# One kernel, two attention layers and two mixtures of experts: new block parts, zeros on another queue, earlier routing, norm rows on ScalarE

## The reference, cut to what is computed

```python
# x: 16 x 256 tokens x 128; 16 heads of 8 dims
x = x + layernorm(softmax_attention(layernorm(x)))       # "soft" layer: q, k, v, o with biases
x = x + layernorm(block0(layernorm(x)))                  # block0 as follows
    h = rmsnorm(X, norm1_w);  X = X + softmax_attention(h) @ wo
    h2 = rmsnorm(X, norm2_w)                             # 4096 tokens
    topw, topi = top_k(softmax(h2 @ router_w), 2)        # 8 experts, 2 for each token
    combine = one_hot(topi) * softmax(topw)
    moe = swiglu(h2, shared) + sum_e combine[:, e] * swiglu(h2, expert e)    # d_ff 256
    return X + moe
x = x + layernorm(power_attention(layernorm(x), W))      # |q.k|^2 with cumulated log gates, causal
x = x + layernorm(capped_moe(layernorm(x)))              # 8 experts, top 2, at most cap tokens each
```

## Time and profile before

| | |
|---|---|
| runs | 1182.12, 1184.04, 1192.7 us; median 1184.04 |
| profiled execution | 1178.53 us, span 1176.7, mean granted clock 0.906 |
| busy, share of the span | PE 1030.3 us (88%), DVE 887.7 (75%), ACT 757.2 (64%), POOL 644.3 (55%) |
| DMA | 75.23 MB in 116022 packets, mean 64 GB/s |

### The profile page before, as it was taken

One profiled execution on the slowest core, in us unless ns is written; L12 is line 12 of the kernel. 1 busy time (PEld: TensorE's weight loads), 2 busy tenths in 40 slices (PEclk: granted clock), 3 DMA queues, 4 the chain that ended last, 5 costly groups with the idle time before them and its releaser, 6 DMA issues. The chain is left out here.

```text
span 1176.7 us, 30894 instructions
## 1 busy us (share of the span) xinstructions
PE 1030.3 (88%) x10524; PEld 615.7 (52%) x10524; DVE 887.7 (75%) x2262; ACT 757.2 (64%) x1638; POOL 644.3 (55%) x707
## 2 busy tenths in 40 slices
PE   4899998999999999885899889888989999938975
PEld 2344444444444444474699765555555566524752
DVE  3899998898898899674544767988888889874223
ACT  1688887888887778831355356757767689733314
POOL 3244444455344444156473647978877678725763
PEclk9999999999999999998899887967777699966998
DMA  5112222212222211001354331111121011132217
GB/s 125 33 47 57 56 56 56 55 52 56 56 56 55 57 43 32 13 24 55 108 149 133 101 86 30 54 51 43 48 61 30 22 47 45 46 133 68 53 61 202
DMA packets 116022, 75.23 MB, mean 64 GB/s; under 512 B 21335, under 2 KB 108064, under 8 KB 115872
## 3 DMA queue, kind: packets, MB, share of 16 engines
q1 hardware_dynamic: 109296, 60.71, 19.1%
q0 software_dynamic: 5888, 12.10, 3.6%
q10 hardware_dynamic: 688, 0.46, 0.1%
HBM read 26.75 MB, written 26.51 MB: 45 GB/s over the span
## 5 line engine op out<-in xcount | busy, mean ns | idle before, releaser
L621 DVE TENSOR_REDUCE mxsS<-scoreS 128x2 f32<-128x512 f32 x512 | 328.6, 685 | 45.7 <-PE scoreS L760 41.2
L509 ACT ACTIVATE PTS<-stS 128x512 f32<-128x512 f32 x512 | 283.5, 592 | 65.8 <-PE stS L764 65.1
L975 POOL TENSOR_TENSOR PTP<-PTP,EP 128x512 f32<-128x512 f32 x128 | 164.7, 1293 | 69.8 <-ACT PTP L1204 68.8
L760 PE MATMUL scoreS<-QK 31*128 31x256 f16 x1024 | 171.3, 280 | 33.5 <-DVE mxsS L621 14.8
L764 PE MATMUL stS<-QK 32*128 32x256 f16 x1024 | 167.9, 277 | 0.9 <-ACT PTS L509 0.9
L685 PE MATMUL pvS<-PTS,Vx 128*32 128x256 f32 x2048 | 140.3, 392 | 0.4
L1396 DVE TENSOR_SCALAR AP<-score_psP 128x768 int32<-128x768 int32 x128 | 121.7, 951 | 21.6 <-PE score_psP L1555 20.6
L1204 ACT ACTIVATE PTP<-AP,epsP 128x768 f32<-128x768 f32 x128 | 119.0, 930 | 25.0 <-DVE AP L1396 24.4
L760 PEld LDWEIGHTS scoreS<-QK 31*128 31x128 f16 x1024 | 53.7, 93 | 154.3 <-DVE mxsS L621 96.3
L382 POOL TENSOR_TENSOR rsS<-veS,halfS 128x2 f32<-128x2 f32 (+1 forms) x32 | 28.0, 874 | 190.2 <-DVE veS L589 103.7
L1216 ACT ACTIVATE EP<-decay_psP 128x512 f32<-128x512 f32 x128 | 75.9, 593 | 49.6 <-PE decay_psP L1537 47.8
(11 more groups left out here) (389 smaller groups left out, 2356.8 us busy)
## 6 DMA issues: line engine op xcount, KB each, us to landing
QK<-HLS SPq DMA_DIRECT2D x384, 32.0 KB, 1.9
QK<-HLP SPq DMA_DIRECT2D x192, 32.0 KB
gsin<-sorted SPq DMA_DIRECT2D x46, 128.0 KB
mixed<-gob SPq DMA_DIRECT2D x46, 128.0 KB, 1.9
sorted<-ggot SPq DMA_DIRECT2D x22, 256.0 KB, 2.4
expert_outputs<-tzero SPq DMA_DIRECT2D x8, 512.0 KB
cgot<-expert_outputs SPq DMA_DIRECT2D x16, 256.0 KB, 5.3
tokens<-XB SPq DMA_DIRECT2D x16, 128.0 KB, 3.1
```

The costliest lines, as they stand in the source:

```text
L509: act.activation(PT[:, n % NPT, :], st_ps[:, (NS * t + n) % 3, :], ACT.Exp, scale=SCALE).then_inc(s_exp, 1)
L621: dve.tensor_reduce(mxs[:, u // 4, :, at], score_ps[:, n % 2, :].rearrange("p (c s) -> p c s", c=TC), AX.X, ALU.max).then_inc(s_max, 1)
L760: scored = pe.matmul(score_ps[:, k, cols], QK[part, new, g, 0, rows], QK[part, new, g, 1, :], start=True, stop=True)
L975: eng.tensor_tensor(w, w, E[:, n % NE, :], ALU.mult).then_inc(s_wd if n % NU in MULT_BY_DVE else s_wp, 1)
```

## The change

- The parts become 3 and 5 blocks: 19 and 27 groups (still 46), 24 and 40 scatters.
- The tables are cleared from ACT's queue: POOL writes a block of zeros at (-3, 0), and ACT issues seven pieces of up to 7 groups at (-3, 0), (-3, 2), (-3, 4), (-2, 0), (-2, 2), (-2, 4), (-1, 0). SP's 24 pieces go.
- Fronts: block 0's goes to soft step 30, blocks 1 and 2 stay in step 31, block 3 moves to units 1 to 3, blocks 4 to 7 some units earlier, on DVE and ACT ahead of the unit's own product and gate. `choose(0)` and `count(0)` are in step 31, `rank(0)` ahead of unit 0 (was unit 2); `choose(1)`, `count(1)`, `rank(1)` are in units 11, 12, 13 (were 14, 15, 16).
- `apply` becomes `shift` (DVE, one 128x4 instruction: minus mean times root), `rows` (ACT, four row scalings with that bias) and `added` (DVE, the add).
- Among the units: block 0 is finished from unit 41 on, blocks 1 and 2 by unit 54, and the head steps of the power layer lie in units 48 to 60. SP's spreads move from 55 and 58 to 51 and 55, its decay spreads from behind the last unit to 59 and 61.
- Block 3 is finished whole in the power layer. Block b of 3 to 7 has its gathers at odd slots of steps 2b-6 and 2b-5, and everything else in step 2b-4: `add0` at slot 0, `add1` 2, `moments` 3, root 4, `shift` 5, `rows` 6, `added` 7.

```diff
-            act.wait_ge(gated.s_sum, 8)
+            act.wait_ge(gated.s_sum, 6)
...
-MOE_PARTS = (4, 4)
+MOE_PARTS = (3, 5)
...
+def nothing_rows(pool):
+    pool.memset(half[:], -0.5).then_inc(s_zero, 1)
+    pool.memset(zero, 0.0).then_inc(s_zero, 1)
+
 def fixed_tables(pool):
-    pool.memset(half[:], -0.5).then_inc(s_zero, 1)
...
-    pool.tensor_tensor(ahead[:], cst[:, C_TRI:C_TRI + P], cst[:, C_IDENT:C_IDENT + P], ALU.subtract)\
-        .then_inc(s_zero, 1)
-    pool.memset(zero, 0.0).then_inc(s_zero, 1)
+    pool.tensor_tensor(ahead[:], cst[:, C_TRI:C_TRI + P], cst[:, C_IDENT:C_IDENT + P], ALU.subtract)
...
 def soft_gpsimd(pool, what, b):
-    if what == "tables":
+    if what == "nothing":
+        nothing_rows(pool)
+    elif what == "tables":
...
 def scatter(pool, h, k):
...
-        pool.wait_ge(s_zero, 3 + 16 * ZERO_PIECES)
+        pool.wait_ge(s_zero, 2 + 16 * ZERO_PIECES)
...
+    moved(0, range(0, 6))
...
-    moved(0, range(0, 4))
+    moved(0, range(6, 9))
...
-    moved(0, range(4, 2 * len(tiles[0])))
+    moved(0, range(9, 2 * len(tiles[0])))
...
-    for b in range(4):
+    for b in range(first_block[1]):
...
+    out_root(pool, first_block[1] - 1)
...
 def front_bank(b):
-    return gate_ps[:, 0, :] if b in (1, 3) else front_ps[:]
+    return down_ps[:, 0, :] if b == 0 else gate_ps[:, 0, :] if b == 2 else front_ps[:]
...
 def turn(pe, b):
...
+        pe.wait_ge(soft.free["PR"], SOFT_STEPS - 3)
+    elif b < 3:
...
-    if b >= 2:
-        reach(pe, s_lg, b - 1 if b < 4 else b)
+    else:
+        pe.wait_ge(s_lg, b)
+    if b == 3:
+        pe.wait_ge(s_rank, RANKED)
...
 def count(pe, h):
...
-    ranks = rank_bank(h)[:, 0:(n + 1) * NE].rearrange("p (t e) -> p t e", e=NE)
+    ranks = front_ps[:, 0:(n + 1) * NE].rearrange("p (t e) -> p t e", e=NE)
...
-        pe.wait_ge(s_zero, 2)
-        pe.wait_ge(soft.s_os, 2 * SOFT_STEPS)
+        pe.wait_ge(s_y, 2)
...
-def rank_bank(h):
-    return turn_ps[:] if h == 0 else front_ps[:]
-
...
 def soft_tensor(pe, what, b):
...
+    elif what == "score":
+        score(pe, b)
+    elif what == "given back":
+        pe.wait_ge(s_lg, b + 1)
...
-        score(pe, b)
+        count(pe, b)
...
 def sorted_turn(pe, s):
...
-        pe.wait_ge(s_rank, RANKED)
+        pe.wait_ge(soft.s_os, 2 * SOFT_STEPS)
...
-TURNS, SCORES, COUNTS = {2: 4, 5: 5, 8: 6, 11: 7}, {4: 4, 7: 5, 10: 6, 13: 7}, {1: 0, 15: 1}
+TURNS, COUNTING = {1: 3, 3: 4, 5: 5, 7: 6, 9: 7}, 12
...
-            pe.wait_ge(s_lg, 4)
+            pe.wait_ge(s_lg, 3)
...
-        if n in SCORES:
-            score(pe, SCORES[n])
-        if n in COUNTS:
-            count(pe, COUNTS[n])
+        if n - 1 in TURNS:
+            score(pe, TURNS[n - 1])
+        if n == COUNTING:
+            count(pe, 1)
...
-def tail_scalar(act, x):
-    evacuate(act, x)
+def norm_rows(act, b):
+    act.wait_ge(s_l, LN_OF * b + 2 * TB + 2)
+    for c in range(TB):
+        last = act.activation(tmp[:, c, :], XB[:, b * TB + c, :], ACT.Identity, bias=nm[:, c:c + 1],
+                              scale=rs[:, c:c + 1])
+    last.then_inc(s_tmp, 1)
+
+def tail_scalar(act, what, x):
+    if what == "evacuate":
+        evacuate(act, x)
+    else:
+        norm_rows(act, x)
...
-        gate(n)
...
+        gate(n)
...
-        if n in (3, 18):
-            tanh_of_logits(act, n // 18)
-        if n in (6, 21):
-            tanh_of_spread(act, n // 21)
+        if n in (3, 16):
+            tanh_of_logits(act, n // 16)
+        if n in (5, 19):
+            tanh_of_spread(act, n // 19)
...
-def norm_apply(dve, b):
-    lk = Link(dve, s_l, LN_OF, b).skip_to(2 * TB + 1)
+def norm_shift(dve, b):
...
-    lk(*[dve.tensor_scalar(tmp[:, c, :], XB[:, b * TB + c, :], mv[:, c, 0:1], rs[:, c:c + 1],
-                           ALU.subtract, ALU.mult) for c in range(TB)])
+    dve.scalar_tensor_tensor(nm[:], mv[:, :, 0], -1.0, rs[:], ALU.mult, ALU.mult).then_inc(s_l, 1)
+
+def norm_added(dve, b):
+    lk = Link(dve, s_l, LN_OF, b).skip_to(2 * TB + 2)
+    dve.wait_ge(s_tmp, b + 1)
...
+    elif what == "shift":
+        norm_shift(dve, b)
...
-        norm_apply(dve, b)
+        norm_added(dve, b)
...
+    rank(dve, 0)
...
-        product(n)
...
-        if n - 1 in SCORES:
-            logits(dve, SCORES[n - 1])
+        if n - 2 in TURNS:
+            logits(dve, TURNS[n - 2])
+        if n == COUNTING + 1:
+            rank(dve, 1)
+        product(n)
...
-        if n == 2:
-            rank(dve, 0)
-        if n == 14:
+        if n == COUNTING - 1:
...
-        if n == 16:
-            rank(dve, 1)
-        if n in (5, 19):
-            weigh(dve, n // 19, 0)
-        if n in (8, 22):
-            weigh(dve, n // 22, 1)
+        if n in (4, 18):
+            weigh(dve, n // 18, 0)
+        if n in (7, 21):
+            weigh(dve, n // 21, 1)
...
-def zeroed(sp, k):
-    h, a, rows = ZERO_PLAN[k]
+def zeroed(act, k):
+    h, a, pairs = ZERO_PLAN[k]
...
-        sp.wait_ge(s_zero, 3)
-    span = tables[h].rearrange("(p r) d -> p r d", p=P)
-    sp.dma_start(span[:, a:a + rows, :], zero[:, 0:rows, :]).then_inc(s_zero, 16)
+        act.wait_ge(s_zero, 2)
+    span = tables[h].rearrange("(p r a) d -> p r (a d)", p=P, a=TC)
+    nothing = zero[:, 0:TC, :].rearrange("p a d -> p (a d)").unsqueeze(1).to_broadcast([P, pairs, TC * D])
+    act.dma_start(span[:, a:a + pairs, :], nothing).then_inc(s_zero, 16)
...
-ZERO_PLAN = [(h, a, min(4, 2 * groups_of(h) - a)) for h in range(len(MOE_PARTS)) for a in range(0, 2 * groups_of(h), 4)]
+ZERO_PLAN = [(h, a, min(7, groups_of(h) - a)) for h in range(len(MOE_PARTS)) for a in range(0, groups_of(h), 7)]
...
     def _(sp):
...
-        soft.sync(sp, {2 + k: functools.partial(gated.zeroed, sp, k) for k in range(ZERO_PIECES)})
-        gated.sync(sp, {55: lambda: power.spread(sp, 0), 58: lambda: power.spread(sp, 1)})
-        for t in range(2):
-            power.spread_decays(sp, t)
+        soft.sync(sp, {})
+        gated.sync(sp, {51: lambda: power.spread(sp, 0), 55: lambda: power.spread(sp, 1),
+                        59: lambda: power.spread_decays(sp, 0), 61: lambda: power.spread_decays(sp, 1)})
...
-        heads = {(1, 7): head("tables", 0), (last, 3): head("squares", 6), (last, 7): head("rows", 6)}
+        heads = {(-3, 0): head("nothing", 0), (1, 7): head("tables", 0), (last, 3): head("squares", 6),
+                 (last, 7): head("rows", 6)}
...
-        tail = {(0, 3): lambda: gated.tail_gpsimd(pool, "root", 3)}
-        for b in range(4, 8):
+        tail = {}
+        for b in range(3, 8):
...
-                tail[2 * b - 7 + k // 4, k % 4 * 2] = gather(b, k)
-            tail[2 * b - 4, 1] = functools.partial(gated.tail_gpsimd, pool, "root", b)
+                tail[2 * b - 6 + k // 4, 1 + k % 4 * 2] = gather(b, k)
+            tail[2 * b - 4, 4] = functools.partial(gated.tail_gpsimd, pool, "root", b)
...
-        def both_fronts(b):
-            return lambda: (gated.soft_scalar(act, b), gated.soft_scalar(act, b + 1))
+        def front(*blocks):
+            return lambda: [gated.soft_scalar(act, b) for b in blocks]
+
+        def zeroed(*pieces):
+            return lambda: [gated.zeroed(act, k) for k in pieces]
+
+        def rows(b):
+            return lambda: gated.tail_scalar(act, "rows", b)
...
         def opening():
-            gated.tail_scalar(act, gated.UNITS - 3)
+            gated.tail_scalar(act, "evacuate", gated.UNITS - 3)
...
-        soft.scalar(act, {(last, 1): both_fronts(0), (last, 5): both_fronts(2)})
-        gated.scalar(act, {53: guest("T", 0), 54: guest("QK", 0), 55: guest("V", 0), 56: guest("T", 1),
-                           57: guest("QK", 1), 58: guest("V", 1), 59: guest("softplus", 0), 60: guest("CS", 0),
-                           61: guest("CS", 1)})
-        power.scalar(act, {(0, 0): opening, (0, 1): lambda: gated.tail_scalar(act, gated.UNITS - 2),
-                           (0, 2): lambda: gated.tail_scalar(act, gated.UNITS - 1)})
+        early = {(-3 + k // 3, k % 3 * 2): zeroed(k) for k in range(ZERO_PIECES)}
+        soft.scalar(act, {**early, (last - 1, 2): front(0), (last, 1): front(1, 2)})
+        gated.scalar(act, {43: rows(0), 47: rows(1), 53: rows(2), 49: guest("T", 0), 50: guest("QK", 0),
+                           51: guest("V", 0), 52: guest("T", 1), 54: guest("QK", 1), 55: guest("V", 1),
+                           56: guest("softplus", 0), 58: guest("CS", 0), 60: guest("CS", 1)})
+        after = {(0, 0): opening, (0, 1): lambda: gated.tail_scalar(act, "evacuate", gated.UNITS - 2),
+                 (0, 2): lambda: gated.tail_scalar(act, "evacuate", gated.UNITS - 1)}
+        after.update({(2 * b - 4, 6): rows(b) for b in range(3, 8)})
+        power.scalar(act, after)
...
-        heads.update({(-3, 5): lambda: load.vector(dve), (last, 2): head("low", 0, 1), (last, 4): head("logits", 0, 1),
-                      (last, 5): head("low", 2, 3), (last, 6): head("square", 6),
```

(42 more changed lines are left out.)

9 lines of the change are left out of this document (6 added, 3 removed).

## The result

The changed kernel takes 1187.07 us in the median of ten runs (1183.88 to 1203.12), the kernel before 1183.69 in ten (1176.62 to 1195.01): a ratio of 1.0064, 95% interval 1.0032 to 1.0095. A later batch gave 1185.45 against 1180.73, 1.0022 (0.9988 to 1.0055). So it is not faster; it is 0 to 1% slower, and the forecast of 1173 us was on the wrong side.

A forecast was written before the change was run, and what follows sets the result against it. It saw gains in TensorE's waits around the sorted units and slow power steps, the later sorted units being full. Terms -16 + 3.5 + 4.5 - 7 - 3 + 7.6 = -10.4 gave 1168.1 us profiled, 1173 median, range 1162 to 1185.

The forecast's parts named there:

- zeros at the opening: Opening: clearing the tables from ACT's queue costs +4.5 us (0 to +9); removing SP's issues is worth 0.
- front of block 0, `choose(0)` earlier: Last soft steps: moving this front to step 30 and `choose(0)` to step 31 was taken at 0 (0 to +3).
- ranks, part 0 of three blocks: Before the first sorted unit: earlier ranks and 24 scatters remove TensorE's 12.0 us wait; -16 us (-18 to -12).
- part 1 of five blocks: Near sorted block 19: 40 scatters in a row on POOL make TensorE wait anew; +3.5 us (0 to +8).
- guests and norms earlier: Last units and power layer entry: starting from unit 41 shortens waits for normalised rows and log gates; -7 us (-12 to 0).
- power step 0: First power step: earlier log gates may let it start at full clock; -3 us (-6 to +3).
- block tail: Power steps 1 to 11: step 1 at 16.8 plus five pairs of 45.8 us; +7.6 us (-18 to +25).
- first rival: Power steps 2 to 11: tail pairs stay cold and dearer, losing from 47.9 us per pair; 1191 us; chance 0.16.
- second rival: Opening: the zeros' bytes are paid in full, 20.8 us in place of 4.5; 1190 us; chance 0.10.
- fourth rival: Before the first sorted unit: the 12 us wait stays, part 0's rows coming 6 us later; 1189 us; chance 0.04.
- third rival: Sorted block 19: a new 8 us wait replaces the old one, some units at half clock; 1183 us; chance 0.13.

The follow-up runs named there:

- c1_after: The changed kernel run once more, unaltered, for a trace nearer its median: 1185.45 us, 1.0022 of the kernel before.
- e1_zact: The kernel before with only the zeros moved, tables cleared from ACT's queue at the opening: 1179.58 us, 0.997 of the kernel before.
- e3_spread: The changed kernel with the power layer's block tail laid as before the change, a block's eight gathers in one step: 1185.72 us, 1.0018 of the kernel before.
- e8_no_gather: The changed kernel without the gathers of blocks 5 to 7, all DVE work kept: 1167.28 us, 0.9858 of the kernel before.
- e2_again: The changed kernel with two more matmuls ahead of each slot of power steps 1 to 11: 1181.83 us, 0.998 of the kernel before.
- e5_norm_dve: The changed kernel with the block norm's row scalings back on DVE at the add's place: 1212.76 us, 1.0234 of the kernel before.
- e12_guests: The changed kernel with block finishing and the power layer's head steps back in units 48 to 61: 1187.53 us, 1.0038 of the kernel before.
- e6_rank: The kernel before with only count(0) and rank(0) earlier, rank(0) ahead of unit 1's product: 0.9989 of the kernel before.
- e11_order: The kernel before with only POOL's order changed, six scatters of part 0 ahead of block 7's squares: 1.0 of the kernel before.
- e13_squares: As e9_order_rank, but with one scatter ahead of block 7's squares instead of six: 1168.14 us, 0.986 of the kernel before.
- e9_order_rank: The kernel before with zeros on ACT, more matmuls in power steps 1 to 10, earlier rank and POOL's new order; parts 4 and 4: 1160.1 us, 0.9806.

## Why the prediction was wrong

The sum by its own terms, c1_after against the trace of before; the trace's total is +7.8, the medians' +3 to +5.

| term | forecast | measured | from |
|---|---|---|---|
| zeros at the opening | +4.5, SP 0 | +6.2 and -11.4 | up to step 0; steps 0 to 29 |
| front of block 0, `choose(0)` earlier | 0 | +3.2 | steps 30, 31, fronts |
| ranks, part 0 of three blocks | -16 | -11.2 and -0.8 | gate 0 to gate 16; units 16 to 20 |
| part 1 of five blocks | +3.5 | +0.1 | units 21 to 40 |
| guests and norms earlier | -7 | +4.9 | unit 41 to power |
| power step 0 | -3 | -3.8 | step 0 |
| block tail | +7.6 | +21.1 | steps 1 to 10 |

**The step that failed first is the block tail in the power layer**, +7.6 forecast and +21.1 measured: the price of a pair, "46.75 - 0.95 = 45.8", and that of step 1, 16.8. Steps 2 to 11 came to 239.8 us in c1_after, 48.0 for a pair, which is the first rival's deciding 47.9. Step 1 took 20.4; the 16.8 was one trace's (20.0 in e1_zact, with the same power layer). The first rival's place and price were the right ones, and it was passed over for an argument that each pair has 0.95 us less DVE work. That argument carried durations from before's places to the new ones. At before's places the change does have four pairs of 45.75 (e3_spread), and loses at the start instead. DVE was busy for 160.9 us in steps 3 to 10 of c1_after, 2.9 more than in before, and the steps took 11.1 more: what was mis-sized is waiting, not work.

"I take the middle because the low clock has a cause that stays", DVE's work, holds for half of a pair. The even steps of e8_no_gather keep that work and stay at 24 us and 0.64. The odd steps do not: without the gathers they go back to 17.1 us and 1.00, and a pair costs 41 instead of 48 to 51. How much of an odd step's 5.6 us is DVE's stall and how much the lower clock behind it stays open, since e2_again raised the clock at a cost in TensorE's time. The size of the term depends on the places, and cannot be worked out from group means at other places.

Rows 8 had shown the stall, a subtraction of 3.43 us while POOL went from a gather into multiplies, and the section on the SBUF ports of the Trainium skill was cited for it, but only for the adds. It was held there that the scaling, with one input, leaves without an effect. The same section of the Trainium skill ("SBUF — State Buffer", "Who interferes with whom") also counts `tensor_scalar` and casts, where their operands allow it, among the instructions that can go into a mode that uses both ports and then lock GpSimd out or wait for it. The runs agree: 988 ns for the scaling and 913 for the 16x256 cast beside POOL (375 and 300). That it is the ports which make them wait fits the rows and is not isolated by a run.

**Guests, -7 forecast, +4.9 measured.** "Some stalls move to units 41 to 47 ...; of 12 I take 7" sized a trade whose two sides are equal. DVE in c1_after, units 41 to 45:

```profile
620.20 1.14 DVE L2531 SCALAR_TENSOR_TENSOR XB<-ggot,gW,XB 128x128 f32<-128x128 f32 x4 [2.05 <-DMA ggot<-mixed,gidx]
628.69 0.69 DVE L2571 TENSOR_TENSOR gprod<-gsg,gup_ps 128x512 f32<-128x512 f32 x1 [2.46 <-ACT gsg L2378]
```

DVE waits 2.05 us for the gathers, as the forecast had it, and then products come late and TensorE with them. The second wait comes by ACT, where the norm rows now stand ahead of a gate:

```profile
626.27 1.65 ACT L2364 ACTIVATE gtmp<-XB,gnm,grs 128x128 f32<-128x128 f32 x4 [2.87 <-DVE gnm L2544]
```

The forecast priced the rows at their 1.5 us and not the 2.87 us for which ACT waits for the shift ahead of them. e5_norm_dve, without rows on ACT, takes 23.8 us in units 41 to 47 instead of 27.4, but 55.7 instead of 48.8 from there to the power layer. In units 48 to 61 the same work stood beside the head steps' own waits. e12_guests shows the whole move, step 0 included, to be worth 0.7 us.

**The opening, +4.5 forecast, -5.2 measured.** The price at the opening was near (6.2). "Their removal is worth 0" was the error. The cover named for it, TensorE's work beside the issues, does not cover an issue that stands ahead of a row on which TensorE waits. The rule of the Trainium skill cited there ("DMA: Bandwidth & Descriptors", "Issuing engines are not separate DMA queues"), that another issuer saves only the issue time, was right in its words: that time, 10.4 us on SP, was what there was to gain, and the soft steps gave back 9.5 to 11.4. The second rival's mechanism came, ACT held ahead of the first turn and the first spread late, but at 6.2 us and not at 20.8. This term erred by 9.7 us on the other side from tail (13.5) and guests (11.9), and hides over a third of what they lost: that the time came within 14 us of the forecast is luck in part.

**Ranks, -16 forecast, -12 measured.** The gap went as said; the rows are in time with 24 scatters. But the reading of the chain was wrong in one place: "their start waits for `rank(0)`" is not what held it, as e6_rank and e11_order show; both the squares and the rank held it, one behind the other. And units 0 to 14, taken at 0, grew by 4.4 us: they were hidden behind the scatters before, and with 24 of them they are the bound. The fourth rival fell. The front moved to step 30 costs 3.2 us in c1_after; over the traces of the changed kernel this is 1 to 5.

**Part 1's wait**, +3.5 forecast, nothing in c1_after, and 1.3 us of TensorE at the first sorted rows of part 1 in e12_guests and e2_again. Its scatters end close to the time at which TensorE comes; units 21 to 40 take 48.4 to 51.1 us over the traces, so 0 to 2.7. The third rival fell. **Step 0** was right in size, and its mechanism is not shown: with the head steps at their old places it takes 22.6 us in before, but 18.5 in e11_order and 18.7 in e13_squares.

The version that beats both kernels leaves parts and guests as before, and takes the zeros on ACT, the earlier rank, POOL's order and the extra matmuls: e9_order_rank, 1160.1 us, 0.9806 (0.9759 to 0.9853).

## What to carry to other kernels

A wait that ends with a row of work is set by the whole row: look at what the queue's first instruction waits for before pricing an earlier release, and at what was hidden behind the row before calling the rest free. An issue on a queue costs its time wherever the next instruction on that queue feeds the bound, however idle the queue is on average. Durations on two engines that contend are not constants: a step moved to another place has to be priced by the neighbours it gets there. A low clock beside a wait need not be its cause, and matmuls that hold the clock up take TensorE's time.

## What the runs showed of the hardware that was not expected

At the opening four DMA issues, three of 896 KB and one of 640, held ACT for 7.1 us. The 24 issues that SP lost gave back about as much as they took (9.5 to 11.4 us for 24 x 0.43). Four DVE scalings of 128x128 with one input from SBUF took 1.13 us beside a gather on POOL, and 3.69 beside two multiplies that POOL ran back to back behind a gather; a cast of 0.28 us took 2.71 beside such a pair. Holding TensorE's clock at 0.87 with matmuls that do no work shortened the steps in which it had been at 0.67 by only 1 us each, and lengthened a step at 1.00 by 1.6.
